# Graph attention kernel, the phase between the two steps: VectorE's passes of tile 1 dealt later among the slots, and z begun by ScalarE

## The chip, the cores and the metric

One core of a Trainium2 chip runs the whole kernel. The metric is device time in microseconds, the median over several executions. Traces come from one profiled execution, and all times in them count from its start. TensorE does the matrix products, VectorE and ScalarE the elementwise work, GpSimd small arithmetic and the accumulating DMAs, SyncE the other DMAs.

## The reference, cut to what matters

```
h = relu(layernorm(x));  S = adj + I
Rf = S / rowsum(S);  Rb = S / colsum(S)        # 3327 x 3327
Xf = Xb = Xa = h;  Z = 0
for s in (0, 1):
    logits = (Xa @ W1[...]) @ W2 @ (Xa @ W3).T
    A = softmax of the largest logits of each row that hold 0.9 of its mass
    Xf, Xb, Xa = Rf @ Xf, Rb @ Xb, A @ Xa
    Z += Xf @ U1[s] + Xb @ U2[s] + Xa @ U3[s]
x = x + layernorm(h + Z) * gamma + beta
```

A second layer follows, which here comes down to a product with given weights. The adjacency has 3327 rows and is padded to 26 tiles of 128 rows; a row of x has 256 columns.

## The kernel before

**Steps and tiles.** A step runs over 26 tiles. For a tile, TensorE makes logits, ScalarE takes exponentials and makes two probes of the threshold, VectorE bisects further (`bisect`, each with one pass over 3327 columns), finds the threshold and the ties (`threshold`, `sum_larger`), and keeps what lies above (`keep`). TensorE then turns the kept rows and multiplies. Beside that it multiplies the adjacency with the rows (`spread`). In the second step a tile has five bisections (`late`), `start_search` stands before them and `row_max` before the exponentials.

**The phase between the steps.** It has two parts: in the first, the attended rows of step one are multiplied with U3 (`third`, `own`, `store_next`). The change lies in the second. It has 26 **slots**, one for each tile t of the spread rows of step one:
- TensorE turns the spread rows of tile t + 2 and makes the products of tile t: two banks of PSUM, four matmuls each, one with U1 and U2 of the first step (I call it the sides' bank), one with those of the second. I call them **products t**. They wait for the banks of slot t - 2: the first for `sides_read`, the second for `both_ready`. After products 5, 9, 13, 17, 21 and 25 a `spread` of the second step's first tile follows.
- ScalarE's `slot(t)` stores the turned rows (L810) and writes the second bank, scaled, to `both` in SBUF (L817, L818). In between stand the exponentials and probes of tiles 0 and 1 of the second step, the counting of ties (L1448), the lifting and the checks of the adjacency (L1459).
- VectorE's `slot(t)` inverts the row sums of tile t + 2 (`invert`) and gathers z of tile t (`gather`): four instructions that add the two halves of the sides' bank and the two halves of `both`, each scaled by `row_inv` or `col_inv`. The second of them frees the sides' bank (`sides_read`).
- GpSimd adds z to memory (`add_own`), with small work of the search between (`make_steps` waits for the first pass of a bisection to have narrowed). There are four z buffers; buffer t % 4 is free again when `z_added` says so.

Each engine runs its own queue in program order, and semaphores are all that ties them. The order among slots and passes on VectorE is written out by hand in `vector`; ScalarE's order of slots, probes and exponentials is written out by hand in `scalar`.

Of the kernel before, what the change touches and what calls it, by code (L numbers as in the profile page):

```python
# [10 lines left out]
ALU = mybir.AluOpType  # L11
# [391 lines left out]
def program(nc, s, x, adjb, adjr, ident_d, W1, W2, W3, U1, U2, U3, gamma, beta, Wks, Wqs, Wvs, WvT, Wo, out):  # L403
# [12 lines left out]
    with whole, ctx:  # L416
# [39 lines left out]
        with ExitStack() as c:  # L456
# [153 lines left out]
            def _(pe):  # L610
# [59 lines left out]
               [f"z_stored{i}" for i in range(4)] + [f"z_added{i}" for i in range(4)] +  # L670
               ["u3_loaded", "u12_loaded", "wqk_loaded", "weights_squared", "att_turned", "att_kept", "keys_done",
                "keys_stored", "queries_done", "queries_stored", "third_done", "third_read", "next_read", "sp_turned",
                "sp_kept", "products_done", "sides_read", "both_ready", "inv_ready", "z_gathered", "dve"]}
        u3 = pair_buffer[:, 0:KT * 2 * D].rearrange("p (k o) -> p k o", k=KT)
        xTg = [pair_buffer[:, (1 + i) * KT * 512:(2 + i) * KT * 512].rearrange("p (k r) -> p k r", k=KT) for i in range(2)]
        att_in = [exps[0][:, i * D:(i + 1) * D] for i in range(4)]
# [104 lines left out]
        def mid_scalar(act):  # L781
            def store_att(t):
                act.wait_ge(mid["att_turned"], t + 1)
                if t >= 8:
                    act.wait_ge(mid["third_done"], t - 7)
                    act.wait_ge(mid["queries_done"], t // 4 - 1)
                act.activation(xTg[t // 4 % 2][:, :, bass.ts(t % 4, P)],
                               banks[t % 2][:, 0:KT * P].rearrange("q (k r) -> q k r", r=P), ACT.Copy
                               ).then_inc(mid["att_kept"], 1)

            def store_keys(g):
                w = s.GROUPS[g][1] * P
                r = (g % 2) * DA
                act.wait_ge(mid["keys_done"], g + 1)
                act.activation(keys_of(g, w), KQ[r:r + DA, 0:w], ACT.Copy).then_inc(mid["keys_stored"], 1)

            def store_queries(g):
                t, w = s.GROUPS[g]
                act.wait_ge(mid["queries_done"], g + 1)
                act.activation(QT[:, t * P:(t + w) * P], QB[:, 0:w * P], ACT.Copy).then_inc(mid["queries_stored"], 1)  # L800

            def store_next(t):
                act.wait_ge(mid["third_read"], t + 1)
                act.activation(h_aug[:, t, 0:D], MB[t % 4][:, D:2 * D], ACT.Copy).then_inc(mid["next_read"], 1)

            def store_spread(t):
                act.wait_ge(mid["sp_turned"], t + 1)
                if t >= 3:
                    act.wait_ge(mid["products_done"], 2 * (t - 2))
                act.activation(spT[t % 3], banks[t % 2][:, 0:KT * P].rearrange("q (k r) -> q k r", r=P), ACT.Copy  # L810
                               ).then_inc(mid["sp_kept"], 1)

            def store_products(t):
                act.wait_ge(mid["products_done"], 2 * t + 2)
                act.wait_ge(mid["inv_ready"], t + 1)
                bank = MB[(T + 2 * t + 1) % 4]
                act.activation(both[:, t, 0:D], bank[:, 0:D], ACT.Copy, scale=row_inv[:, t:t + 1])  # L817
                act.activation(both[:, t, D:2 * D], bank[:, D:2 * D], ACT.Copy, scale=col_inv[:, t:t + 1]  # L818
                               ).then_inc(mid["both_ready"], 1)

            def square():
                act.wait_ge(mid["wqk_loaded"], 32)
                act.activation(wqk, wqk, ACT.Square, accum_out=found[:, 1:2]).then_inc(mid["weights_squared"], 1)
                act.wait_ge(mid["weights_squared"], 1)
            return MidScalar(store_att, store_keys, store_queries, store_next, store_spread, store_products, square)

        def mid_vector(dve):
            chain = Steps(dve, mid["dve"])

            def own(t):  # L830
                dve.wait_ge(mid["third_done"], t + 1)
                if t >= 4:
                    dve.wait_ge(mid[f"z_stored{t % 4}"], t // 4 * 16)
                dve.tensor_tensor(z_out[t % 4], MB[t % 4][:, 0:D], h_aug[:, t, 0:D], ALU.add
                                  ).then_inc(mid["third_read"], 1)

            def invert(t):
                dve.wait_ge(mid[f"spread_loaded{t % 4}"], (t // 4 + 1) * 16)
                chain.did(dve.tensor_scalar(row_sum[:, t:t + 1], spread_in[t % 4][:, D:SW], 1e-12, None, ALU.max))
                chain.wait()  # L840
                dve.reciprocal(row_inv[:, t:t + 1], row_sum[:, t:t + 1]).then_inc(mid["inv_ready"], 1)

            def gather(t):
                z = z_out[t % 4]
                sides = MB[(T + 2 * t) % 4]
                dve.wait_ge(mid["inv_ready"], t + 1)
                dve.wait_ge(mid["products_done"], 2 * t + 1)
                if t < 4:
                    dve.wait_ge(mid[f"z_stored{t}"], stores_in(t))
                else:  # L850
                    dve.wait_ge(mid[f"z_added{t % 4}"], t // 4 * 16)
                chain.did(dve.tensor_scalar(z, sides[:, 0:D], row_inv[:, t:t + 1], None, ALU.mult))
                chain.wait()
                dve.scalar_tensor_tensor(z, sides[:, D:2 * D], col_inv[:, t:t + 1], z, ALU.mult, ALU.add
                                         ).then_inc(mid["sides_read"], 1)
                dve.wait_ge(mid["sides_read"], t + 1)
                dve.wait_ge(mid["both_ready"], t + 1)
                chain.did(dve.scalar_tensor_tensor(z, both[:, t, 0:D], row_inv[:, t:t + 1], z, ALU.mult, ALU.add))
                chain.wait()
                dve.scalar_tensor_tensor(z, both[:, t, D:2 * D], col_inv[:, t:t + 1], z, ALU.mult, ALU.add  # L860
                                         ).then_inc(mid["z_gathered"], 1)
            return MidVector(own, invert, gather)

        def step(number):
# [4 lines left out]
            if True:  # L869
# [993 lines left out]
                def vector(dve, parts):  # L1863
# [276 lines left out]
                    if first_step:  # L2140
                        row_max(0)
                    else:
                        pad = keys_of(NG - 1, NP - (NG - 1) * 512)[:, N - NP:]
                        for i in range(2):
                            dve.wait_ge(first.sem[f"spread_stored{i}"], 16 * (T // 2))
                        for t in range(T):
                            parts.own(t)
                            if t == T - 5:
                                dve.wait_ge(mid["keys_stored"], NG)
                                chain.did(dve.tensor_tensor(fold[:, :], ident[:, 0:DA], ident[:, DA:P], ALU.add))  # L2150
                                chain.did(dve.memset(pad, 0.0))
                                chain.wait()
                                dve.tensor_reduce(key_sum[:, :], KTr[:, :], AX.X, ALU.add
                                                  ).then_inc(sem["keys_summed"], 1)
                            if t == T - 3:
                                dve.wait_ge(sem["keys_folded"], 1)
                                dve.tensor_scalar(pad, KQ[0:DA, 0:1], 1.0 / N, None, ALU.mult
                                                  ).then_inc(sem["keys_ready"], 1)
                        parts.invert(0)
                        parts.invert(1)  # L2160
                        slots(0, 2)
                        row_max(0)
                        slots(2, 5)
                        row_max(1)
                        slots(5, 8)
                        start_search(0)
                        slot(8)
                        for k in range(late):
                            bisect(0, k)
                            slot(9 + k)  # L2170
                        threshold(0, lambda: slot(14))
                        sum_larger(0)
                        slot(15)
                        start_search(1)
                        slot(16)
                        bisect(1, 0)
                        slot(17)
                        bisect(1, 1)
                        slot(18)
                        keep(0)  # L2180
                        slot(19)
                        bisect(1, 2)
                        slots(20, T)
                        bisect(1, 3)
                        row_max(2)
                        bisect(1, 4)
                        threshold(1)
                        sum_larger(1)
# [117 lines left out]
```

## Time and profile before

| | us |
|---|---|
| median of 3 runs (lowest, highest) | 2310.26 (2309.46, 2310.35) |
| the profiled execution | 2308.43 |
| its span | 2306.6 |
| busy: TensorE / VectorE / ScalarE / GpSimd | 2132.9 / 2046.8 / 1943.6 / 883.9 |
| mean granted clock of TensorE, as a share of full | 0.981 |
| the second part of the phase, first products to last spread | 1005.67 to 1153.4 |

The busy times say how full an engine is over the whole; no engine is full throughout, and what a change in one stage is worth shows in the rows of that stage.

### The profile page before, as it was taken

To read this page: it belongs to the slowest core of one execution; us is meant where nothing else is said; L and a number is where in the kernel's file an instruction comes from. 1 tells how busy PE (TensorE), PEld (TensorE's weight loads), DVE (VectorE), ACT (ScalarE), POOL (GpSimd) and SP (SyncE) were. 2 spreads that over 40 slices of the span, in tenths; PEclk is the share of its full clock that TensorE was granted. 3 is DMA by queue.
4 is the path that set the end of the run, shared out by engine and by line. 5 is a ranking of instruction groups with operands and counts; after the bars stand their busy time and mean duration, and the time that the engine had idled before them with its cause. 6 is when DMAs were issued, how large, how long until landed. Compare 5 with 4: busy or idle time off the path is not lost.

```text
span 2306.6 us, 26328 instructions
## 1 busy us (share of the span) xinstructions
PE 2132.9 (92%) x8250; PEld 1376.1 (60%) x8250; DVE 2046.8 (89%) x3721; ACT 1943.6 (84%) x2849; POOL 883.9 (38%) x1247
## 2 busy tenths in 40 slices
PE   7599999999999998997999999999999999999975
PEld 4377777777777777443356555555555555555554
DVE  5699999999999998148859999999999999999995
ACT  4899999999999995257389899999999899899844
POOL 2134443344433442002224444444444444444432
PEclk9699999999999999999999999999999999999988
DMA  7255544555445552432321221221221221122242
GB/s 242 82 124 137 113 98 110 128 122 113 98 117 128 115 111 59 115 93 39 56 56 52 52 52 43 52 58 37 52 59 37 52 58 43 48 57 52 46 118 71
DMA packets 85168, 190.05 MB, mean 82 GB/s; under 512 B 12193, under 2 KB 65056, under 8 KB 85024
## 3 DMA queue, kind: packets, MB, share of 16 engines
q0 software_dynamic: 26208, 61.37, 16.8%
q1 hardware_dynamic: 56496, 125.48, 16.4%
q10 hardware_dynamic: 2320, 1.48, 0.2%
q8 instruction: 67, 1.10, 0.2%
q14 instruction: 77, 0.63, 0.1%
HBM read 154.19 MB, written 34.10 MB: 82 GB/s over the span
## 4 chain that ended last, share of the span: by engine, by line
DVE 45%; PE 4%; issue 1%; ACT 1%; POOL 0%; DVEq 0%; ACTq 0%; POOLq 0%
DVE junk L1941 19%; DVE small L1988 4%; DVE logits L1980 4%; DVE logits L2113 4%; DVE small L1884 4%; PE bank L1118 2%; DVE small L1969 1%; DVE small L1972 1%; DVE QT L2057 1%; PE bank L776 1%; DVE small L1993 1%; DVE small L1996 1%; PE bank L1180 1%; PE bank L1144 0%; PE bank L1100 0%
## 5 line engine op out<-in xcount | busy, mean ns | idle before, releaser
L1941 DVE SCALAR_TENSOR_TENSOR junk<-logits,small,expd 128x3327 uint8<-128x3327 f32 x184 | 677.9, 3684 | 4.7
L1144 PE MATMUL bank<-h_aug,turns 128*128 128x256 f32 x2704 | 629.8, 380 | 0.1
L1118 PE MATMUL bank<-both,pair 128*128 128x512 f32 x1352 | 610.9, 596 | 17.6 <-ACT sides L1494 17.6
L1144 PEld LDWEIGHTS bank<-h_aug,turns 128*128 128x128 f32 x2704 | 499.2, 190 | 95.2 <-issue 30.3
L1118 PEld LDWEIGHTS bank<-both,pair 128*128 128x128 f32 x1352 | 250.8, 190 | 302.2 <-issue 260.8
L1118 PE MATMUL bank<-h_aug,both 128*128 128x257 f32 x1352 | 316.7, 384 | 2.0 <-ACT sides L1477 1.6
L1118 PEld LDWEIGHTS bank<-h_aug,both 128*128 128x128 f32 x1352 | 251.0, 190 | 63.7 <-issue 26.9
L1100 PE MATMUL bank<-KTr,QT 64*128 64x512 f32 (+1 forms) x728 | 246.4, 613 | 44.3 <-ACT logits L1341 40.4
L1401 ACT ACTIVATE junk<-expd,small 128x3327 int8<-128x3327 f32 x88 | 270.1, 3069 | 1.5
L1407 ACT ACTIVATE junk<-expd,small 128x3327 int8<-128x3327 f32 x88 | 270.4, 3073 | 0.3
L1741 POOL TENSOR_TENSOR small<-small 128x1 f32<-128x1 f32 x52 | 14.4, 277 | 571.5 <-DVE small L2013 571.5
L1470 ACT ACTIVATE turns<-bank 128x512 f32<-128x512 f32 (+1 forms) x364 | 188.6, 562 | 47.5 <-PE bank L1134 41.8
L1134 PE MATMUL bank<-ident,logits 128*128 128x128 f32 x1352 | 191.1, 277 | 39.4 <-DVE logits L2113 29.3
L1134 PEld LDWEIGHTS bank<-ident,logits 128*128 128x128 f32 x1352 | 160.1, 142 | 100.2 <-DVE logits L2113 39.8
L1988 DVE MAX8 small<-logits 128x8 f32<-128x416 f32 (+1 forms) x416 | 209.9, 577 | 0.0
L1448 ACT ACTIVATE junk<-logits,small 128x3327 int8<-128x3327 f32 x52 | 159.4, 3066 | 49.0 <-DVE small L2005 49.0
L1100 PEld LDWEIGHTS bank<-KTr,QT 64*128 64x128 f32 x728 | 90.0, 188 | 183.0 <-ACT logits L1341 104.9
L1980 DVE SCALAR_TENSOR_TENSOR logits<-logits,small,expd 128x3327 f32<-128x3327 f32 x44 | 162.6, 3694 | 1.5
L1348 ACT ACTIVATE expd<-logits,small 128x3327 f32<-128x3327 f32 x44 | 135.0, 3068 | 33.7 <-DVE small L1886 33.6
L1341 ACT ACTIVATE logits<-bank 128x512 f32<-128x512 f32 (+1 forms) x286 | 145.4, 575 | 20.7 <-PE bank L1100 20.6
L2113 DVE SCALAR_TENSOR_TENSOR logits<-logits,small,expd 128x3328 f32<-128x3328 f32 x42 | 154.7, 3684 | 4.7 <-DVE small L2110 0.5
L1706 POOL TENSOR_SCALAR small<-small 128x1 f32<-128x1 f32 x52 | 41.0, 788 | 264.2 <-ACT expd L1348 242.9
(259 smaller groups left out, 3120.2 us busy)
## 6 DMA issues: line engine op xcount, KB each, us to landing
both<-adj_turned SPq DMA_DIRECT2D x52, 832.0 KB, 6.8
both<-adj_turned POOLq DMA_DIRECT2D x52, 832.0 KB, 9.4
pair<-adj_turned SPq DMA_DIRECT2D x52, 832.0 KB, 4.5
z<-sides POOLq DMA_DIRECT2D x78, 128.0 KB, 3.1
spread<-sides POOLq DMA_DIRECT2D x26, 128.5 KB, 3.7
turns<-spread SPq DMA_DIRECT2D x26, 128.5 KB, 2.1
attended<-att_out SPq DMA_DIRECT2D x26, 128.0 KB, 8.7
expd<-attended SPq DMA_DIRECT2D x26, 128.0 KB, 2.1
```

What stands on the lines that cost most here:

```text
L1100: pe.matmul(logits_bank(i)[:, 0:w], QT[r:r + DA, bass.ts(t, P)], keys_of(n, w), start=True, stop=True).then_inc(sem["logits_done"], 1)
L1118: done = pe.matmul(SX[:, 0:width], half(t, h)[:, bass.ts(jj, P)], rows_of(j), start=(j == 0), stop=(j == T - 1))
L1134: last = pe.transpose(TB[i % NTB][:, bass.ts(b, P)], kept[:, bass.ts(g + b, P)], ident[:, :])
L1144: last = pe.matmul(AB[:, 0:D], attT[i % 4][:, b, :], h_aug[:, g + b, 0:D], start=(g + b == 0), stop=(g + b == T - 1))
L1401: chain.did(act.activation(junk2[:, 0:N], e, ACT.Relu, bias=at, scale=-0.5, accum_out=col(t, "tail")))
L1407: chain.did(act.activation(junk2[:, 0:N], e, ACT.Sign, bias=at, scale=-0.5, accum_out=col(t, "side")))
L1448: act.activation(junk2[:, 0:N], me, ACT.Sign, bias=col(t, "tau"), scale=-1.0, accum_out=col(t, "less")).then_inc(sem["ties_counted"], 1)
L1470: act.activation(attT[i % 4][:, 0:w, :], TB[i % NTB][:, 0:w * P].rearrange("q (b r) -> q b r", r=P), ACT.Relu).then_inc(sem["turned_stored ...
L1941: chain.did(dve.scalar_tensor_tensor(junk[:, 0:N], logits[t % 3][:, 0:N], col(t, "cand"), expd[t % NE][:, 0:N], ALU.is_gt, ALU.mult, accum ...
L1980: chain.did(dve.scalar_tensor_tensor(me[:, 0:N], logits[t % 3][:, 0:N], col(t, "cand"), expd[t % NE][:, 0:N], ALU.is_le, ALU.mult, accum_o ...
L1988: chain.did(dve.max(winners(t)[:, 8 * n:8 * n + 8], me[:, at:min(at + NP // SEGMENTS, N)]))
L2113: dve.scalar_tensor_tensor(kept, kept, col(t, "sharetau"), expd[t % NE][:, :], ALU.add, ALU.min).then_inc(sem["kept_ready"], 1)
```

## The change

It does two things, both inside the slots. The first term of z, the row half of `both` scaled by `row_inv`, is now written to the z buffer by ScalarE, right behind the two stores of `both` (L825 of the new file). VectorE adds the other three terms. ScalarE takes over the wait for the z buffer, and VectorE waits for `z_begun` where it waited for the products. On VectorE the passes of tile 1 and the keeping of tile 0 stand later among the slots, mostly with two or more slots between them.

```diff
--- before.py
+++ after.py
@@ -817,6 +817,13 @@
                 act.activation(both[:, t, 0:D], bank[:, 0:D], ACT.Copy, scale=row_inv[:, t:t + 1])
                 act.activation(both[:, t, D:2 * D], bank[:, D:2 * D], ACT.Copy, scale=col_inv[:, t:t + 1]
                                ).then_inc(mid["both_ready"], 1)
+                act.wait_ge(mid["both_ready"], t + 1)
+                if t < 4:
+                    act.wait_ge(mid[f"z_stored{t}"], stores_in(t))
+                else:
+                    act.wait_ge(mid[f"z_added{t % 4}"], t // 4 * 16)
+                act.activation(z_out[t % 4], both[:, t, 0:D], ACT.Copy, scale=row_inv[:, t:t + 1]
+                               ).then_inc(mid["z_begun"], 1)
@@ -844,19 +851,12 @@
                 z = z_out[t % 4]
                 sides = MB[(T + 2 * t) % 4]
                 dve.wait_ge(mid["inv_ready"], t + 1)
-                dve.wait_ge(mid["products_done"], 2 * t + 1)
-                if t < 4:
-                    dve.wait_ge(mid[f"z_stored{t}"], stores_in(t))
-                else:
-                    dve.wait_ge(mid[f"z_added{t % 4}"], t // 4 * 16)
-                chain.did(dve.tensor_scalar(z, sides[:, 0:D], row_inv[:, t:t + 1], None, ALU.mult))
+                dve.wait_ge(mid["z_begun"], t + 1)
+                chain.did(dve.scalar_tensor_tensor(z, sides[:, 0:D], row_inv[:, t:t + 1], z, ALU.mult, ALU.add))
                 chain.wait()
                 dve.scalar_tensor_tensor(z, sides[:, D:2 * D], col_inv[:, t:t + 1], z, ALU.mult, ALU.add
                                          ).then_inc(mid["sides_read"], 1)
                 dve.wait_ge(mid["sides_read"], t + 1)
-                dve.wait_ge(mid["both_ready"], t + 1)
-                chain.did(dve.scalar_tensor_tensor(z, both[:, t, 0:D], row_inv[:, t:t + 1], z, ALU.mult, ALU.add))
-                chain.wait()
                 dve.scalar_tensor_tensor(z, both[:, t, D:2 * D], col_inv[:, t:t + 1], z, ALU.mult, ALU.add
                                          ).then_inc(mid["z_gathered"], 1)
@@ -2170,17 +2170,17 @@
                         threshold(0, lambda: slot(14))
                         sum_larger(0)
-                        slot(15)
+                        slots(15, 17)
                         start_search(1)
-                        slot(16)
+                        slot(17)
                         bisect(1, 0)
-                        slot(17)
+                        slots(18, 20)
+                        keep(0)
+                        slot(20)
                         bisect(1, 1)
-                        slot(18)
-                        keep(0)
-                        slot(19)
+                        slots(21, 23)
                         bisect(1, 2)
-                        slots(20, T)
+                        slots(23, T)
                         bisect(1, 3)
                         row_max(2)
                         bisect(1, 4)
```

VectorE behind the first pass of tile 1, whose last instruction is L1955, before the change: one slot (17), then the next pass (L1941).

```order
L1955 SCALAR_TENSOR_TENSOR small1<-small1 128x1
L839 TENSOR_SCALAR row_sum<-turns 128x1
L841 RECIPROCAL row_inv<-row_sum 128x1
L852 TENSOR_SCALAR sides<-bank3,row_inv 128x256
L854 SCALAR_TENSOR_TENSOR sides<-bank3,col_inv,sides 128x256
L858 SCALAR_TENSOR_TENSOR sides<-both,row_inv,sides 128x256
L860 SCALAR_TENSOR_TENSOR sides<-both,col_inv,sides 128x256
L1941 SCALAR_TENSOR_TENSOR junk,small1<-logits1,small1,expd1 128x3327
```

The same place after the change: two slots (18 and 19), then the keeping of tile 0 (from L2105).

```order
L1955 SCALAR_TENSOR_TENSOR small1<-small1 128x1
L846 TENSOR_SCALAR row_sum<-turns 128x1
L848 RECIPROCAL row_inv<-row_sum 128x1
L855 SCALAR_TENSOR_TENSOR sides<-bank6,row_inv,sides 128x256
L857 SCALAR_TENSOR_TENSOR sides<-bank6,col_inv,sides 128x256
L860 SCALAR_TENSOR_TENSOR sides<-both,col_inv,sides 128x256
L846 TENSOR_SCALAR row_sum<-turns 128x1
L848 RECIPROCAL row_inv<-row_sum 128x1
L855 SCALAR_TENSOR_TENSOR sides<-bank3,row_inv,sides 128x256
L857 SCALAR_TENSOR_TENSOR sides<-bank3,col_inv,sides 128x256
L860 SCALAR_TENSOR_TENSOR sides<-both,col_inv,sides 128x256
L2105 RECIPROCAL small0<-small0 128x1
```

A gather has three instructions where it had four, and two banks are freed before VectorE's next long instruction where it was one.

VectorE around bisect(1, 2), the pass L1941, before the change: it stands behind slot 19, and slots 20 and 21 follow without a pass.

```order
L860 SCALAR_TENSOR_TENSOR sides<-both,col_inv,sides 128x256
L1941 SCALAR_TENSOR_TENSOR junk,small1<-logits1,small1,expd1 128x3327
L1969 TENSOR_SCALAR small1<-small1 128x1
L1972 SCALAR_TENSOR_TENSOR small1<-small1 128x1
L839 TENSOR_SCALAR row_sum<-turns 128x1
L841 RECIPROCAL row_inv<-row_sum 128x1
L852 TENSOR_SCALAR sides<-bank6,row_inv 128x256
L854 SCALAR_TENSOR_TENSOR sides<-bank6,col_inv,sides 128x256
L858 SCALAR_TENSOR_TENSOR sides<-both,row_inv,sides 128x256
L860 SCALAR_TENSOR_TENSOR sides<-both,col_inv,sides 128x256
```

The same pass after the change: it stands behind slot 22, and slots 23, 24 and 25 are left.

```order
L860 SCALAR_TENSOR_TENSOR sides<-both,col_inv,sides 128x256
L1941 SCALAR_TENSOR_TENSOR junk,small1<-logits1,small1,expd1 128x3327
L1969 TENSOR_SCALAR small1<-small1 128x1
L1972 SCALAR_TENSOR_TENSOR small1<-small1 128x1
L846 TENSOR_SCALAR row_sum<-turns 128x1
L848 RECIPROCAL row_inv<-row_sum 128x1
L855 SCALAR_TENSOR_TENSOR sides<-bank3,row_inv,sides 128x256
L857 SCALAR_TENSOR_TENSOR sides<-bank3,col_inv,sides 128x256
L860 SCALAR_TENSOR_TENSOR sides<-both,col_inv,sides 128x256
L855 SCALAR_TENSOR_TENSOR sides<-bank6,row_inv,sides 128x256
```

Slot 23's gather, which frees the bank of products 25, now has this pass ahead of it.

## Rows read from the trace of the kernel before

**Rows 1.** Busy time by engine in one stretch, instructions in brackets, then clock and DMA

```profile
core 0: us, PE busy (x) PEld busy (x) DVE busy (x) ACT busy (x) POOL busy (x), PEclk, DMA share, GB/s
1053.00:1127.00 74.00, 54.64 (x135) 24.17 (x133) 70.37 (x149) 43.41 (x76) 22.24 (x38) 0.93 0.25 40
```

**Rows 2.** The chain that ended last, in order of time: start, us, what

```profile
1126.94 3.67 PE bank L776 x8
...
1206.45 3.63 DVE small L1884
```

**Rows 3.** Waits from 1003 to 1206 us: in total, times, longest

```profile
PE bank L776 <- DVE sides L854: 19.4, 8, 6.2
```

**Rows 4.** Timeline of VectorE: start, us, instruction, in brackets idle time before it

```profile
1031.33 0.49 DVE L858 SCALAR_TENSOR_TENSOR sides<-both,row_inv,sides 128x256 f32<-128x256 f32 x1 [2.79 <-ACT both L818]
...
1050.42 0.15 DVE L1909 TENSOR_SCALAR s_mask<-small 128x1 int32<-128x1 f32 x1 [2.90 <-ACT small L1430]
...
1052.74 0.15 DVE L839 TENSOR_SCALAR row_sum<-turns 128x1 f32<-128x1 f32 x1
...
1053.05 0.48 DVE L852 TENSOR_SCALAR sides<-bank,row_inv 128x256 f32<-128x256 f32 x1
1053.57 0.48 DVE L854 SCALAR_TENSOR_TENSOR sides<-bank,col_inv,sides 128x256 f32<-128x256 f32 x1
...
1055.01 3.68 DVE L1941 SCALAR_TENSOR_TENSOR junk<-logits,small,expd 128x3327 uint8<-128x3327 f32 x1
...
1060.37 0.48 DVE L854 SCALAR_TENSOR_TENSOR sides<-bank,col_inv,sides 128x256 f32<-128x256 f32 x1
...
1061.81 3.68 DVE L1941 SCALAR_TENSOR_TENSOR junk<-logits,small,expd 128x3327 uint8<-128x3327 f32 x1
...
1066.09 0.15 DVE L839 TENSOR_SCALAR row_sum<-turns 128x1 f32<-128x1 f32 x1
```

**Rows 5.** Timeline of ScalarE between 1019 and 1116 us

```profile
1019.84 0.47 ACT L818 ACTIVATE both<-bank,col_inv 128x256 f32<-128x256 f32 x1
1020.51 1.08 ACT L1341 ACTIVATE logits<-bank 128x512 f32<-128x512 f32 x2 [0.21 <-PE bank L1100]
...
1030.75 0.48 ACT L818 ACTIVATE both<-bank,col_inv 128x256 f32<-128x256 f32 x1
1031.11 0.88 ACT L1341 ACTIVATE logits<-bank 128x512 f32<-128x512 f32 x2
...
1050.01 0.39 ACT L1430 ACTIVATE small<-small 128x1 f32<-128x1 f32 x1
...
1102.77 0.47 ACT L817 ACTIVATE both<-bank,row_inv 128x256 f32<-128x256 f32 x1 [10.39 <-PE bank L776]
...
1103.50 3.07 ACT L1448 ACTIVATE junk<-logits,small 128x3327 int8<-128x3327 f32 x1
...
1114.24 1.68 ACT L1459 ACTIVATE junk<-pair,neg_below_one 128x1664 int8<-128x1664 f32 x1
```

**Rows 6.** Timeline of TensorE: the products of slots 11, 16, 17, 18, 22, 23 to 25

```profile
1061.00 3.67 PE L776 MATMUL bank<-logits,turns 128*128 128x512 f32 x8 [1.63 <-DVE sides L854]
...
1097.60 5.13 PE L776 MATMUL bank<-logits,turns 128*128 128x512 f32 x8 [6.16 <-DVE sides L854]
...
1102.79 3.60 PE L776 MATMUL bank<-logits,turns 128*128 128x512 f32 x8
...
1109.87 3.60 PE L776 MATMUL bank<-logits,turns 128*128 128x512 f32 x8
...
1134.10 3.60 PE L776 MATMUL bank<-logits,turns 128*128 128x512 f32 x8
...
1137.76 10.47 PE L776 MATMUL bank<-logits,turns 128*128 128x512 f32 x24
```

**Rows 7.** Timeline of VectorE behind the slots

```profile
1162.41 3.62 DVE L1884 TENSOR_REDUCE small<-logits 128x1 f32<-128x3327 f32 x1 [8.04 <-ACT logits L1341]
...
1194.33 0.15 DVE L1909 TENSOR_SCALAR s_mask<-small 128x1 int32<-128x1 f32 x1 [13.15 <-ACT small L1430]
```

**Rows 8.** DMA issues of the whole run: KB each, us from issue to landing

```profile
z<-sides POOLq DMA_DIRECT2D x78, 128.0 KB, 3.1
```

More of the change, by code:

```diff
@@ L672, in program @@
                 "keys_stored", "queries_done", "queries_stored", "third_done", "third_read", "next_read", "sp_turned",
-                "sp_kept", "products_done", "sides_read", "both_ready", "inv_ready", "z_gathered", "dve"]}
+                "sp_kept", "products_done", "sides_read", "both_ready", "inv_ready", "z_begun", "z_gathered", "dve"]}
         u3 = pair_buffer[:, 0:KT * 2 * D].rearrange("p (k o) -> p k o", k=KT)
```

## The prediction

> **What bounds the kernel now.** I read the busy time of a stretch first, then the chain of work that ended last, then the timelines of VectorE, ScalarE and TensorE between 1003 and 1206 us. The change touches only the second phase between the steps; what surrounds it has the same instructions. VectorE is busy for 70.4 of the 74 us in the middle of that phase, TensorE for 54.6 [rows 1]. The chain that ended last passes from VectorE to TensorE at 1126.94, when the products of slot 21 start, stays on TensorE, and is back on VectorE at 1206.45, from where the regular loop over tiles runs on VectorE [rows 2]. So an end of the slots that comes X us earlier on TensorE moves everything behind it by X, as long as nothing else becomes late there.
>
> TensorE in turn waits for VectorE in eight slots, 19.4 us together, because gather's second instruction frees the bank that the products two slots later need [rows 3]. That sum is no forecast: the gaps can only be closed as far as VectorE really comes earlier.
>
> **Prices of the parts.** On VectorE, inverting takes 0.30 us (1052.74 to 1053.05). The four instructions of a gather start 0.52 apart, and the last leaves after 0.40, so 1.96 us (1053.05 to 1055.01). Without one instruction a gather costs 1.44. The bank is free 1.00 us after a gather starts, before and after, since it is the second instruction that frees it. A bisection pass of tile 0 or 1 takes 4.28 (1061.81 to 1066.09). A wait of VectorE for ScalarE costs 0.10 beyond the end of ScalarE's instruction (1030.75 + 0.48 to 1031.33) [rows 4].
>
> On ScalarE the new instruction is not in the trace. It reads 256 columns from SBUF. From the nearest rows that read SBUF, 1.68 us for 1664 columns and 3.07 for 3327 (the last two of these rows), a column costs 0.84 ns, which gives 0.50 for 256; the copies from PSUM take 0.48. I take 0.50; the ends are 0.45 and 0.60. It must wait for L818 to finish (0.50 after that one's start, a release included), and lets the next start some 0.38 after its own start, where L818 today lets it start after 0.36 (1030.75 to 1031.11). So a slot gets 0.50 + 0.38 - 0.36 = about 0.53 us longer on ScalarE [rows 5].
> The Trainium skill (VectorE: DVE Perf Modes, The TRN2 errata) lists a ScalarE instruction that reads SBUF with 224 fixed cycles and one that reads PSUM with 172. That is 0.04 us more for the new one, and speaks against moving work there; by its figures the instruction would be 0.40 us, the rows say 0.50, and five slots at 0.10 less would make the time below 0.5 us shorter.
>
> **The sum, first part: ScalarE is full, and the search of tile 0 starts later.** From the exponentials of tile 0 (1021.5) to the second probe's last result at 1050.01 no row of ScalarE has idle time ahead of it, as the three here that lie in that stretch show, and VectorE's start_search(0) at 1050.42 waits 2.90 for that result [rows 4, 5]. Five slots (3 to 7) lie in that stretch: 5 x 0.53 = 2.65. Of slots 0 to 2 only the last counts: L818 at 1019.84 would let a copy start 0.36 later, the copy of logits starts at 1020.51, so 0.32 of the 0.53 is covered and 0.21 is left. VectorE's search of tile 0 starts 2.9 us later, at 1053.3. The same lag makes the products of slots 8 and 9 wait about a microsecond each for a bank, since now ScalarE's hand-off stands before gather; TensorE has over 1.6 us of slack at slot 11 and more behind it, so this costs nothing.
>
> **Second part: the gathers give it back.** Slots 8 to 13 lie on VectorE between there and the bank of slot 14: 6 x 0.52 = 3.1. The products of slot 16, which wait for that bank, start at 1097.60 [rows 6]; now 0.2 earlier, at 1097.4. I keep their 5.13 us there (3.60 elsewhere): the granted clock had fallen after 6.2 us of waiting, and that wait stays nearly the same.
>
> **Third part: VectorE's passes no longer stand between the banks.** From products 16 to products 22 TensorE took 36.50 (1097.60 to 1134.10), most of it idle or slow. With the passes dealt later, the bank of each slot is free in time. Slot 16's z is begun at 1104.0, so the gather ends at 1105.5, start_search(1) (2.3, as 1050.42 to 1052.74) at 1107.8; gather 17 waits for ScalarE, which counts ties first (3.07), until 1108.7 and frees its bank at 1109.7, where products 19 need it at 1113.3; the pass follows, gather 18 frees at 1115.9 (needed 1117.0); gather 19 waits for its z until 1118.5 and frees at 1119.5 (needed 1120.7); keep(0), as long as a pass, and gather 20: 1125.4 (needed 1127.7). So TensorE runs through, at its own intervals: 5.19 with the slow stretch (16 to 17), 7.08 with a spread in it (17 to 18), three of 3.66 (as 1134.10 to 1137.76), and 7.08 again (21 to 22), 30.3 in all [rows 6]. Products 22 start at 1127.7, 6.4 earlier.
>
> **Fourth part: some is lost at the end.** Products 22 end at 1131.3. ScalarE follows after 0.04 (1102.77 behind 1097.60 + 5.13), needs 0.37 + 0.50 + 0.50 until z is begun, and VectorE starts after 0.10: gather 22 runs from 1132.8 to 1134.3. Now bisect(1, 2) comes (4.28, to 1138.6), then 0.30 and 1.00 until the bank of slot 23 is free at 1139.9. A release of TensorE costs another 0.15 (as 1060.37 + 0.48 to 1061.00): products 25 start at 1140.0. Before, they were the last of three in a row that began at 1137.76 and took 10.47: 1137.76 + 10.47 - 3.60 = 1144.6 [rows 4, 6]. **That is 4.6 us earlier**, of the 6.4 that stood at slot 22.
>
> **Behind the slots.** Nothing there is late. VectorE's last gather now waits for z (1145.0), and with the last pass it is done at about 1150.8; the logits of tile 2 that it needs next come at 1162.41 - 4.6 = 1157.8, a wait of 7.0 of the 8.04 today. ScalarE's search of tile 2, for which VectorE idles 13.15 us, starts behind TensorE's turned blocks and moves along [rows 7]. ScalarE's new wait for z_added reaches four slots back: a store lands 3.1 us after its issue [rows 8], while four slots take over 14 us (4 x 3.66 at the fastest), so it is free; queued behind it would be the turned spread and the bank's release. GpSimd now holds add_own(17) until bisect(1, 0) has narrowed (about 1114.5), and slot 21 asks for it at 1125.
>
> The profiled execution took 2308.43 with a span of 2306.6, so the span should be 2302.0 and that execution about 2303.8. The median of the runs is 2310.26, 1.8 above the profiled one; 2310.26 - 4.6 = **2305.7**.
>
> **Rivals.**
> Full saving: all 26 missing instructions count, 13.5 us, 2296.8. For it: VectorE is nearly full in the middle. Against: only the six gathers of the second part stand on the path, and ScalarE takes their gain first. 5%.
> The clock: the granted clock decides what products 16 cost. If the wait before them no longer lets it fall, 1.5 us more is gained: 2304.2. Or waits of some 2 us, which now stand before products 11 to 13, let it fall there too; 1.5 each, which VectorE's passes cover, so no change. The Trainium skill (TensorE: Matmul & The Clock Gate, HAM oscillation) describes bursts that run cold again after each wait; by it the second case could come, still without a price. 15%, nearly all for the shorter time.
> ScalarE becomes the bound (the other side): its chain from products to a begun z sets both start_search(0) and, at slots 16 to 22, the gathers. Each 0.1 us more for it costs 0.5 up to start_search(0) and 0.1 at slot 22. At 0.77 us more per slot, 1.3 in all, the 4.6 are gone; at 1.6 more, as when z's accumulation were awaited in several slots, the kernel is 5.0 slower, 2315.3. For it: ScalarE has no idle time up to 1050. Against: the fixed part is known within 0.1, and the awaited stores are old. 10%, half of it slower by more than 0.2%.
> Forecast as summed: 70%, with 3.0 to 6.2 us gained, 2304.1 to 2307.3.
>
> **Chances.** A measurement of this kernel can tell about 0.2%, 4.6 us, from no change, and the forecast stands on that line. Faster by over 0.2%: half of the forecast (0.34), the clock 0.13, the full saving 0.05, so 0.52. Within 0.2%: 0.36 + 0.02 + 0.05 = 0.43. Slower: 0.05. The range must hold the clock case and part of the third rival: 2302.5 to 2309.5, with the full saving and the worst of the third left out.
>
> **What the changed profile would show.** Start_search(0) at about 1053.3 after a wait for ScalarE; products 16 at 1097.4 at a low clock; no wait of TensorE from there to products 24; a wait of about 1.5 us before products 25 for gather's second instruction, at 1140.0; row_max(3) near 1201.8. L825 at 0.50 us. The forecast fails if L825 or its release is dearer, if ScalarE's hand-off holds back a bank behind slot 16, or if the tail from 1148 on does not move as one piece.

## The result, and the profile after

| | before | with the change |
|---|---|---|
| median of 11 runs, us (lowest, highest) | 2310.35 (2309.46, 2312.92) | 2305.74 (2303.86, 2307.84) |
| the profiled execution, us | 2308.43 | 2306.07 |
| its span, us | 2306.6 | 2304.3 |

The medians differ by 4.6 us, where 4.6 was forecast. The ratio is 0.9978, with a 95% interval from 0.9969 to 0.9987, so the runs alone say 3.0 to 7.2 us: that the two numbers agree to a tenth is luck.

The two spans differ by 2.3 us only, and that is no contradiction. The slots of the profiled execution with the change began 1.6 us later than before (1007.30 for products 0, against 1005.67), after a first step that has the same instructions. That makes 3.9 us by the span. Another 0.7 lies behind row_max(3), where the rest of the kernel took 1100.9 us, against 1100.2 before; in the nine profiles of this document that rest lies between 1099.2 and 1101.7, so 0.7 can't be read as an effect. What the change does is therefore read as distances from products 0:

| us behind products 0 | before | forecast | with the change |
|---|---|---|---|
| start_search(0) | 44.75 | 47.6 | 47.68 |
| products 16 | 91.93 | 91.7 | 91.18 |
| products 22 | 128.43 | 122.0 | 121.93 |
| products 25 | 138.96 | 134.3 | 134.20 |
| row_max(3) | 200.78 | 196.1 | 196.10 |

The timeline of TensorE with the change, products 8, 9, 11 to 13, 15 to 17, 19, 22, 23 to 24, and 25, answers to [rows 6]. In brackets is the idle time before a row and what ended it.

```profile
1047.63 3.67 PE L776 MATMUL bank<-logits,turns 128*128 128x512 f32 x8 [1.03 <-DVE sides L857]
...
1052.22 3.67 PE L776 MATMUL bank<-logits,turns 128*128 128x512 f32 x8 [0.70 <-DVE sides L857]
...
1064.97 3.67 PE L776 MATMUL bank<-logits,turns 128*128 128x512 f32 x8 [1.78 <-DVE sides L857]
...
1070.97 5.37 PE L776 MATMUL bank<-logits,turns 128*128 128x512 f32 x8 [2.11 <-DVE sides L857]
...
1076.96 3.67 PE L776 MATMUL bank<-logits,turns 128*128 128x512 f32 x8 [0.41 <-DVE sides L857]
...
1088.97 3.67 PE L776 MATMUL bank<-logits,turns 128*128 128x512 f32 x8 [1.04 <-DVE sides L857]
...
1098.48 5.56 PE L776 MATMUL bank<-logits,turns 128*128 128x512 f32 x8 [5.61 <-DVE sides L857]
...
1104.10 3.60 PE L776 MATMUL bank<-logits,turns 128*128 128x512 f32 x8
...
1114.84 3.60 PE L776 MATMUL bank<-logits,turns 128*128 128x512 f32 x8
...
1129.23 3.60 PE L776 MATMUL bank<-logits,turns 128*128 128x512 f32 x8
...
1133.04 7.10 PE L776 MATMUL bank<-logits,turns 128*128 128x512 f32 x16
...
1141.50 3.67 PE L776 MATMUL bank<-logits,turns 128*128 128x512 f32 x8 [1.35 <-DVE sides L857]
```

Behind 1098.48 no products wait for a bank until those of slot 25. The new waits before products 8 and 9 are the ones that ScalarE's hand-off was to cause (in the kernel with z from slot 8 on, below, they are gone), and they are covered by the slack in front of products 11. Products 12 took 5.37 us behind a wait of 2.11, at a mean granted clock of 0.68 of full; the wait before products 13 shrank to 0.41 with it, from 2.65 before the change. The last wait, 1.35 us, is bisect(1, 2)'s.

VectorE and ScalarE with the change. First VectorE's start_search(0), gather 22 and gather 23 with the pass between them, and what follows behind the slots, as in [rows 4] and [rows 7]:

```profile
1054.98 0.15 DVE L1909 TENSOR_SCALAR s_mask<-small 128x1 int32<-128x1 f32 x1 [2.39 <-ACT small L1430]
...
1134.35 0.48 DVE L855 SCALAR_TENSOR_TENSOR sides<-bank,row_inv,sides 128x256 f32<-128x256 f32 x1 [0.68 <-ACT sides L825]
...
1135.79 3.68 DVE L1941 SCALAR_TENSOR_TENSOR junk<-logits,small,expd 128x3327 uint8<-128x3327 f32 x1
...
1140.35 0.48 DVE L855 SCALAR_TENSOR_TENSOR sides<-bank,row_inv,sides 128x256 f32<-128x256 f32 x1
1140.87 0.48 DVE L857 SCALAR_TENSOR_TENSOR sides<-bank,col_inv,sides 128x256 f32<-128x256 f32 x1
...
1159.37 3.62 DVE L1884 TENSOR_REDUCE small<-logits 128x1 f32<-128x3327 f32 x1 [6.99 <-ACT logits L1341]
...
1191.28 0.15 DVE L1909 TENSOR_SCALAR s_mask<-small 128x1 int32<-128x1 f32 x1 [13.14 <-ACT small L1430]
...
1203.40 3.62 DVE L1884 TENSOR_REDUCE small<-logits 128x1 f32<-128x3327 f32 x1 [0.92 <-ACT logits L1341]
```

Then ScalarE in a slot that the search of tile 0 leaves no room around, as in [rows 5]. The new instruction starts 0.51 us after L818 and lets the next start after another 0.41, so a slot costs ScalarE 0.56 more; 0.53 was taken.

```profile
1045.36 0.48 ACT L818 ACTIVATE both<-bank,col_inv 128x256 f32<-128x256 f32 x1
1045.87 0.51 ACT L825 ACTIVATE sides<-both,row_inv 128x256 f32<-128x256 f32 x1
1046.28 3.06 ACT L1401 ACTIVATE junk<-expd,small 128x3327 int8<-128x3327 f32 x1
```

Two other views say the same. VectorE now waits for ScalarE's new instruction, 33.3 us in all, while TensorE's waits for the banks fell from 19.4 us to 14.0. And of the same 74 us as in [rows 1] TensorE is busy for 63.1 us where it was for 54.6, VectorE for 64.4 where it was for 70.4 (the stretch is the same on the clock of each profile, and the slots lie 1.6 us later in the second):

```profile
DVE sides L855 <- ACT sides L825: 33.3, 11, 6.7
...
PE bank L776 <- DVE sides L857: 14.0, 8, 5.6
```

```profile
1053.00:1127.00 74.00, 63.06 (x155) 28.22 (x154) 64.38 (x154) 54.95 (x103) 21.88 (x40) 0.93 0.31 57
```

The chain that ended last, cut to the end of the slots (start, us, what), has just the links of the fourth part of the forecast: products 22 on TensorE, three instructions of ScalarE, gather 22, the pass, two instructions of gather 23, products 25.

```profile
1129.40 3.45 PE bank L776 x8
...
1133.74 0.52 ACT sides L825
...
1135.39 0.48 DVE sides L860
1135.88 3.62 DVE junk L1941 x2
...
1140.87 0.50 DVE sides L857
1141.36 0.14 issue
1141.50 3.67 PE bank L776 x8
1145.17 5.15 PE bank L1118 x12
```

### The profile page after: what moved, and what is told of

It is laid out like the page before. It is cut to its first block, busy times and chain, and to the rows that moved or that the text cites. A ratio compares the mean times of both kernels' runs of the same rounds, so it can differ in the third digit from the quotient of the medians.

```text
span 2304.3 us, 26328 instructions
## 1 busy us (share of the span) xinstructions
PE 2135.7 (93%) x8250; PEld 1377.2 (60%) x8250; DVE 2034.3 (88%) x3695; ACT 1956.4 (85%) x2875; POOL 883.7 (38%) x1247
## 4 chain that ended last, share of the span: by engine, by line
DVE 46%; PE 5%; issue 2%; ACT 1%; POOL 0%; DVEq 0%; ACTq 0%; POOLq 0%
DVE junk L1941 20%; DVE small L1988 4%; DVE logits L1980 4%; DVE small L1884 4%; DVE logits L2113 4%; PE bank L1118 2%; PE bank L776 1%; DVE small L1969 1%; DVE small L1972 1%; DVE QT L2057 1%; DVE small L1993 1%; DVE small L1996 1%; PE bank L1180 1%; PE bank L1144 0%; PE bank L1100 0%
## 5 line engine op out<-in xcount | busy, mean ns | idle before, releaser
L1941 DVE SCALAR_TENSOR_TENSOR junk<-logits,small,expd 128x3327 uint8<-128x3327 f32 x184 | 677.9, 3684 | 4.7
```

The source lines that it names most:

```text
L1941: chain.did(dve.scalar_tensor_tensor(junk[:, 0:N], logits[t % 3][:, 0:N], col(t, "cand"), expd[t % NE][:, 0:N], ALU.is_gt, ALU.mult, accum ...
```

## The experiments

The theory: up to products 16 the time is set by ScalarE (search of tile 0) and then by VectorE's gathers, from there to products 22 by TensorE, and products 25 by the pass that was dealt late. The rivals: the saved instruction counts in full; ScalarE's new work is a loss that the dealing covers; or it costs nothing, since ScalarE has room.

Seven kernels were run, five to eleven times each. The kernel before was timed beside them: the first four share one set of its runs (median 2310.72), the last three another on another chip (median 2310.09), and the change has its own (2310.35). So between the sets the ratios compare better than the medians. A ratio's interval is 1.8 to 2.7 parts in a thousand wide, 4 to 6 us, so that the intervals of most neighbours in the table overlap; the distances from products 0, from one profiled execution each, carry the argument.

| kernel | median, us | ratio, 95% | products 16 | products 25 | row_max(3) |
|---|---|---|---|---|---|
| before | 2310.35 | | 91.93 | 138.96 | 200.78 |
| the change | 2305.74 | 0.9978 (0.9969 to 0.9987) | 91.18 | 134.20 | 196.10 |
| z only | 2307.50 | 0.9987 (0.9978 to 0.9996) | 91.17 | 137.14 | 198.98 |
| dealt only | 2305.57 | 0.9977 (0.9968 to 0.9986) | 91.92 | 135.15 | 197.05 |
| z twice in slots 3 to 7 | 2307.26 | 0.9986 (0.9977 to 0.9995) | 93.86 | 137.21 | 199.11 |
| z from slot 8 on | 2302.99 | 0.9965 (0.9951 to 0.9978) | 88.38 | 132.62 | 194.52 |
| late pass | 2303.93 | 0.9973 (0.9963 to 0.9984) | 91.13 | 132.64 | 194.47 |
| z from 8, late pass | 2301.17 | 0.9962 (0.9948 to 0.9975) | 88.38 | 129.45 | 191.28 |
| and threshold split | 2297.14 | 0.9949 (0.9935 to 0.9962) | 84.46 | 126.33 | 188.17 |

**One part alone: z.** ScalarE begins z as in the change; VectorE's order is that of before.

```diff
-                        slots(15, 17)
+                        slot(15)
                         start_search(1)
-                        slot(17)
+                        slot(16)
                         bisect(1, 0)
-                        slots(18, 20)
-                        keep(0)
-                        slot(20)
+                        slot(17)
                         bisect(1, 1)
-                        slots(21, 23)
+                        slot(18)
+                        keep(0)
+                        slot(19)
                         bisect(1, 2)
-                        slots(23, T)
+                        slots(20, T)
```

> ScalarE begins z in every slot, but VectorE's passes stay where they were before the change. Measure in the trace: from products 0 to products 25, which took 138.96 us before and 134.20 with the whole change. My theory: the search of tile 0 starts 2.9 later, the bank of slot 14 comes about 0.7 earlier as with the whole change, and between slots 16 and 22 the old passes cost TensorE less because each gather is 0.52 shorter; 135.5 to 135.9, so the kernel 3.1 to 3.5 us faster than before, near 2307. Rival, that the saved instruction alone counts in full: 26 x 0.52, 13.5 us, 2297. Rival, that ScalarE's added work is a loss unless the dealing covers it: the kernel is 1 to 3 us slower than before.

Start_search(0) came 47.68 us behind products 0 and products 16 91.17 behind them, as with the whole change. Products 25 came at 137.14, above the 135.5 to 135.9 of the theory. TensorE's timeline of this kernel, products 20 and 21:

```profile
1117.19 3.67 PE L776 MATMUL bank<-logits,turns 128*128 128x512 f32 x8 [0.86 <-DVE sides L857]
...
1123.14 5.37 PE L776 MATMUL bank<-logits,turns 128*128 128x512 f32 x8 [2.06 <-DVE sides L857]
```

Products 21 started 117.8 us behind products 0, within 0.2 of the walk behind the estimate, and then ran 1.7 us longer than elsewhere, at the low clock. The mean granted clock was 0.68 in products 21, behind a wait of 2.06, and 1.00 in products 20. That accounts for the miss. In this profile the gain at products 25 is 1.8 us; the median is 3.2 us below before (0.9 to 5.1 by the interval), the theory's size. The full saving (2297) and the loss are both out.

**The other part alone: the dealing.** The diff is the last hunk of the change, applied to the kernel before.

> VectorE's passes dealt later as in the change, but the gather has its old four instructions and ScalarE does not begin z. My theory: nothing changes up to products 16 (91.9 us behind products 0); behind them TensorE runs through to products 24, and products 25 wait for the gather behind bisect(1, 2); 134.6 from products 0 to products 25, 4.4 less than before, about 2306. The two parts then give 3.3 and 4.4 alone and 4.7 together, since they close the same gaps. Rival, that both parts add up: this one gives only the difference, 1.3 us, 2309.

2305.57 us: in the medians the dealing alone can't be told from the whole change. Alone the parts measured 5.2 and 3.2 us, together 4.6; at products 25 of the profiles they are 3.8 and 1.8, together 4.8, and z alone would have 3.5 without the slow products 21. So they don't add up, and the rival with 2309 is out: a gain of 1.3 us lies outside the interval of 3.2 to 7.4. Products 25 came 0.55 later than expected. Products 16 took 0.75 more in that execution, 5.88 us where the kernel before took 5.13, and that covers it.

```profile
1101.60 5.88 PE L776 MATMUL bank<-logits,turns 128*128 128x512 f32 x8 [4.47 <-DVE sides L854]
```

**ScalarE's suspected cost, doubled.** In slots 3 to 7 ScalarE writes the first term of z twice; the result is the same.

```diff
...
+                if 3 <= t < 8:
+                    act.activation(z_out[t % 4], both[:, t, 0:D], ACT.Copy, scale=row_inv[:, t:t + 1]
+                                   ).then_inc(mid["z_twice"], 1)
+                    act.wait_ge(mid["z_twice"], t - 2)
                 act.activation(z_out[t % 4], both[:, t, 0:D], ACT.Copy, scale=row_inv[:, t:t + 1]
                                ).then_inc(mid["z_begun"], 1)
```

> The whole change, and in slots 3 to 7 ScalarE writes the first term of z twice, with a wait between: some 0.52 us more in each of those slots and nowhere else. My theory, in which ScalarE is full there and sets the start of the search of tile 0: start_search(0) 5 x 0.52 = 2.6 later (50.3 us behind products 0 instead of 47.7), products 16 and products 25 2.6 later too (136.8), the kernel 2.6 us slower than with the change, near 2308.4. Rival, that ScalarE has room: at most 0.5 later anywhere, and the time of the change.

Start_search(0) came at 50.38, 2.70 later than with the change; products 16 at 93.86, 2.68 later; products 25 at 137.21, 3.01 later, of which 0.33 is again products 16 (5.89 against 5.56). In this profile ScalarE's time in those five slots passes one for one to everything behind. The median is 1.5 us above that of the change (2307.26), 1.1 below the expected one, and the intervals of the two ratios overlap: the timed runs agree in sign only, and the profile gives the size.

**ScalarE's cost, taken away where ScalarE is full.** VectorE gathers with four instructions in slots 0 to 7, and ScalarE begins z from slot 8 on. The cut shows ScalarE's side; VectorE's gather has the same condition.

```diff
+Z_FROM = 8
...
-                act.wait_ge(mid["both_ready"], t + 1)
-                if t < 4:
-                    act.wait_ge(mid[f"z_stored{t}"], stores_in(t))
-                else:
-                    act.wait_ge(mid[f"z_added{t % 4}"], t // 4 * 16)
+                if t < Z_FROM:
+                    return
+                act.wait_ge(mid["both_ready"], t + 1)
+                act.wait_ge(mid[f"z_added{t % 4}"], t // 4 * 16)
...
```

> The whole change, but in slots 0 to 7 VectorE gathers with its four instructions as before, and ScalarE begins z from slot 8 on. My theory: start_search(0) back at 44.75 behind products 0, six shorter gathers then bring products 16 to 88.8, and everything behind moves along: products 25 at 131.5, 7.5 less than before and 2.7 less than with the change; 2303.0. Rival, that ScalarE's new place on the way to a bank costs later on: no better than the change, 2305.7.

2302.99 us, the expected 2303.0. Start_search(0) is back at 44.73, and products 16 come at 88.38 (88.8 expected). Products 25 came 1.1 later than expected: products 16 came 0.4 earlier and lasted 6.61 us in the profiled execution, 1.5 more than the 5.13 before. They still came 1.6 us before those of the change and 2.5 before those of the dealing alone; the intervals of the ratios overlap, so this order rests on the profiles.

```profile
1096.20 6.61 PE L777 MATMUL bank<-logits,turns 128*128 128x512 f32 x8 [5.34 <-DVE sides L865]
```

**The late pass.** The whole change, with bisect(1, 2) behind all slots.

```diff
                         bisect(1, 1)
-                        slots(21, 23)
+                        slots(21, T)
                         bisect(1, 2)
-                        slots(23, T)
                         bisect(1, 3)
```

> The whole change, with bisect(1, 2) moved from behind slot 22 to behind slot 25, ahead of bisect(1, 3). My theory, in which that pass holds back the bank of slot 23: the wait before products 25 (1.35 us) goes, and TensorE runs through to the last spread; from products 0 to products 25 132.6 instead of 134.20, near 2304.1. VectorE has two passes behind the slots now, 4.3 more, and its wait for the logits of tile 2 shrinks from 6.99 to about 4.3, so it isn't late. Rival, that what is cut there comes back at row_max(2): the time of the change.

2303.93 us, 1.8 below the change by the medians and 1.2 by the ratios, with intervals that overlap. The profile shows where. Products 23 to 25 now run in one piece, and products 25 come at 1132.55 + 10.54 - 3.60 = 1139.49, which is 132.64 behind products 0 (1006.85). VectorE still waits at row_max(2), for 2.69 us. I had written 4.3 there; that was a slip, 6.99 less one pass of 4.3 is 2.7. Row_max(3) came 1.6 earlier with the rest, so the rival is out as far as there. Behind it, the rest of the kernel took 1101.3 to 1101.7 us in the three profiles with the late pass, and 1099.2 to 1101.0 in the six others; whether part of the gain is lost there again was not tested.

```profile
1132.55 10.54 PE L776 MATMUL bank<-logits,turns 128*128 128x512 f32 x24
```

```profile
1157.28 3.62 DVE L1884 TENSOR_REDUCE small<-logits 128x1 f32<-128x3327 f32 x1 [2.69 <-ACT logits L1341]
```

**Both.** The last two edits together.

> Both together: z begun by ScalarE from slot 8 on, and bisect(1, 2) behind slot 25. My theory: the two act at different places and add up; from products 0 to products 25 130.9 instead of 132.6 with the first alone, near 2301.3, VectorE's wait for the logits of tile 2 still about 4. Rival: the second brings nothing on top of the first, 2303.

2301.17 us. Products 25 come at 129.45 instead of the expected 130.9, because products 16 took 5.13 us here and 6.61 in the execution that the estimate started from. Without that difference the late pass brings 1.7 us here and 1.6 on the change: in the profiles the two edits add up. The medians have the expected size, but by their intervals the two kernels with z from slot 8 can't be told apart. VectorE's wait for the logits of tile 2 is 2.69 again, where 4 was written.

**The longest wait, cut.** The kernel with both, and in addition: in the threshold of tile 0 slot 14 stands between the pass and the MAX instructions, slot 15 behind these.

```diff
-                    def threshold(t, meanwhile=None):
+                    def threshold(t, between=None, meanwhile=None):
...
+                        if between is not None:
+                            between()
                         for n in range(SEGMENTS):
...
-                        threshold(0, lambda: slot(14))
+                        threshold(0, lambda: slot(14), lambda: slot(15))
                         sum_larger(0)
-                        slots(15, 17)
+                        slot(16)
```

> As the one with both, and in the threshold of tile 0 slot 14 stands between its long pass and the eight MAX instructions, slot 15 behind these (both slots stood one stretch later). My theory: the longest wait of TensorE, 5.3 us before products 16, is cut to about 1.5, a second one of about 1.5 appears before products 17, and the products there may no longer run at the low clock, which cost 1.5 to 3.0 us in all runs so far. From products 0 to products 25 127.0 if those products keep the low clock, 125.5 to 124.5 if not; 2297.5, or 2295 to 2296. Rival, that VectorE or ScalarE is late behind it since tile 0's threshold ends 3.5 us later in its order: no gain on the one with both, 2301.3.

2297.14 us, the fastest kernel here, 0.51% under the one before (0.38% to 0.65%); its five runs all lie below the five of the kernel with both. TensorE's timeline, products 15, 16 and 17:

```profile
1084.83 3.67 PE L777 MATMUL bank<-logits,turns 128*128 128x512 f32 x8 [1.19 <-DVE sides L865]
...
1090.39 3.67 PE L777 MATMUL bank<-logits,turns 128*128 128x512 f32 x8 [1.67 <-DVE sides L865]
...
1096.03 3.67 PE L777 MATMUL bank<-logits,turns 128*128 128x512 f32 x8 [1.75 <-DVE sides L865]
```

The wait of 5.3 us is now two of 1.7, and products 16 take 3.67 us at a granted clock of 1.00. For that case 124.5 to 125.5 had been expected; products 25 come at 126.33, 0.8 later, with 127.0 expected at the low clock. Against the kernel with both that is 3.1 us earlier, of which 1.5 is the shorter products 16; most of the rest is the waits, 3.4 where they were 5.3. The two were changed by one edit and are told apart only by these rows.

## Why the prediction was right, point by point

- **ScalarE is full up to start_search(0): +2.9.** Measured +2.93, of which 0.21 was there when the exponentials of tile 0 began, as summed for slot 2 (16.03 us behind products 0, against 15.82). Shown by the doubling (+2.70 for five more instructions) and by taking it away (back to 44.73).
- **Six gathers give 3.1 back, products 16 0.2 earlier.** They came 0.75 earlier. The error is in the term's size. The kernel before had one extra gap of about 0.3 us on VectorE, in front of gather 12 (the row below), which the forecast took as fixed and which is gone; why it was there is open. The rest, some 0.25, is that inverting, from its start to the start of the gather, now takes 0.26 us, as 1063.56 to 1063.82, where it took 0.30, and seven of them lie on this way.
- **Products 16 keep 5.13 us.** They took 5.56. The two misses, 0.55 for one and 0.43 against it, cancelled, and that products 22 came within 0.1 of the forecast is luck to that extent. The forecast's "3.60 elsewhere" is not so: products 20 took 5.37 us in the kernel before, behind a wait of 2.66 (the other row below).
- **TensorE runs through from products 16 to 22: 30.3 us.** 30.75 with the longer products 16, and no wait on the way. The forecast calls most of the 36.50 us before "idle or slow"; by its own intervals it was 7.7 of them, of which the change took 5.7 and products 16 keep the rest. The sum didn't use the phrase.
- **1.8 is lost again before products 25, by the late pass.** The wait is there (1.35), and moving the pass behind the slots removed it and gave 1.6 in the profile and 1.8 in the medians (1.2 by the ratios).
- **The rest moves as one piece.** Row_max(3) came 4.68 earlier, products 25 4.76. VectorE's waits behind the slots were 6.99 (7.0 said), 13.14 and 0.92, and no row shows ScalarE waiting for a z buffer, as said.
- **The rivals.** The full saving is out: z alone gave 3.2 of 13.5 us. ScalarE as the bound is real as a mechanism, at its place up to slot 8, and worth 2.8 us of loss at products 16 (88.38 without it, 91.18 with it) inside a net gain. Of the two clock cases the second came: products 12 ran slow behind a wait of 2.11, and VectorE's passes covered it. The first did not, but the clock's price at products 16 was 1.5 to 3.0 us in eight profiles, and in the one profile with a shorter wait it was gone.

The two rows of the kernel before, gather 12 on VectorE and products 20 on TensorE:

```profile
1079.84 0.48 DVE L852 TENSOR_SCALAR sides<-bank,row_inv 128x256 f32<-128x256 f32 x1 [0.30 <-DVE row_inv L841]
...
1120.45 5.37 PE L776 MATMUL bank<-logits,turns 128*128 128x512 f32 x8 [2.66 <-DVE sides L854]
```

What the forecast had not asked is what either part is worth by itself. Both work on the same waits, and done in all slots ScalarE's begin of z adds nothing to the dealing that the medians show: in the profiles it loses 2.9 us in slots 2 to 7 and gains 3.7 behind them, which leaves 0.75 at products 16. Begun at slot 8 it keeps the gain without the loss, 3.5 us at products 16 (88.38, against 91.92 with the dealing alone).

## What to carry to other kernels

A term moved from a busy engine to another one is worth what it saves where the first sets the pace, less what it costs where the second does; both can be true in one phase, and then the move should be made in only a part of the loop. Deal long passes by asking, at each one, whose buffer stands behind it in the queue: for bisect(1, 2) the place behind all slots was better than the one behind slot 22, since the engine would have waited there anyway. When two edits close the same gap, measure them apart before keeping both.

## What the runs showed of the hardware beyond that

The same eight matmuls of products 16 took 5.13, 5.56, 5.17, 5.88, 5.89, 6.61, 5.56 and 5.13 us in eight profiles, each after a wait of 4.5 to 6.2 us, and 3.67 in the ninth, with a wait of 1.67. The mean granted clock over them was 0.71, 0.66, 0.71, 0.62, 0.62, 0.55, 0.66 and 0.71 of full (1.00 in the last), so they ran partly at the lower of its two levels. Time multiplied by granted clock is 3.6 to 3.7 in all nine: the clock accounts for the whole difference. Products behind waits of 2.1 and 2.7 us sometimes ran slow too (5.37, mean clock 0.68), sometimes not, in the same kernel. From one profile to another this shifts what lies behind by up to 1.5 us, which is a third of the effect studied. The start of the slots, behind a first step that is the same in all kernels, lay between 1005.37 and 1009.68 us; the cause is open. Both together are why distances within a profile, and medians over many runs, were used and single spans were not.
